# Gated expert rows added by scatter DMA straight into the output, tile by tile, in a two-stage FFN kernel

## The reference

```python
# stage A
h = gelu(x @ fc1_w.T + fc1_b)                      # 128 -> 512
y = concat([h @ fc2_w.T + fc2_b,                   # 96 shared outputs
            h @ experts_w[idx[seq]].T + experts_b[idx[seq]]])   # 32, one of 16 by sequence
# stage C
scores = y @ router_w.T                            # 8 experts
top_v, top_i = top_k(scores, 2);  w = softmax(top_v)
out = x + sum_e (gelu(y @ w1[e].T) @ w2[e].T) * w_e
```

## Time and profile before

| | us |
|---|---|
| median of 3 runs | 344.18 |
| lowest, highest | 340.74, 346.32 |
| span of the profiled execution | 320.1 |
| median minus span | 24.1 |
| POOL busy with the 64 scatters of stage A | 68.0 |
| POOL busy with the 80 scatters of stage C | 86.9 |

### The profile page before, as it was taken

One profiled execution on the slowest core, in us unless ns is written; L12 is line 12 of the kernel. 1 busy time (PEld: TensorE's weight loads), 2 busy tenths in 40 slices (PEclk: granted clock), 3 DMA queues, 4 the chain that ended last, 5 costly groups with the idle time before them and its releaser, 6 DMA issues.

```text
span 320.1 us, 5181 instructions
## 1 busy us (share of the span) xinstructions
PE 235.2 (73%) x1138; PEld 180.7 (56%) x1138; DVE 188.4 (59%) x471; ACT 178.5 (56%) x265; POOL 185.9 (58%) x203
## 2 busy tenths in 40 slices
PE   7974999979877326799999999798977979700000
PEld 2653776657655201578888888697856868600000
DVE  2568988578576470077776775465454665501880
ACT  4888577578461230296767666476555555401830
POOL 3009587777777774005776777565736656662660
PEclk9999799979979957699999999899999979955555
DMA  4395234329611153557775776847856664214981
GB/s 133 101 333 177 73 96 141 104 75 273 200 43 59 51 187 132 208 181 240 244 253 200 248 288 240 314 173 250 265 194 250 199 234 156 98 33 133 361 248 46
DMA packets 32611, 57.90 MB, mean 181 GB/s; under 512 B 5544, under 2 KB 15920, under 8 KB 32594
## 3 DMA queue, kind: packets, MB, share of 16 engines
q1 hardware_dynamic: 23778, 43.76, 39.1%
q0 software_dynamic: 4608, 8.54, 8.3%
q10 hardware_dynamic: 4208, 5.42, 6.0%
HBM read 20.56 MB, written 13.02 MB: 105 GB/s over the span
## 4 chain that ended last, share of the span: by engine, by line
PE 23%; issue 22%; POOL 22%; DMA 18%; DVE 5%; ACT 4%; SPq 3%; POOLq 1%; DVEq 0%; ACTq 0%
POOL slots L583 15%; PE hp L359 11%; DMA results<-rows,back_now 10%; PE dn L372 8%; POOL results L603 4%; DMA slots<-y_rows,slot 4%; PE dx L1069 2%; POOL ffn L624 2%; PE tr L1084 1%; DMA ffn<-results 1%; ACT hs L397 1%; ACT hid L387 1%; SPq L450 1%; DMA ffn_raw<-in_w2T 1%; DVE ffn L983 1%
## 5 line engine op out<-in xcount | busy, mean ns | idle before, releaser
L603 POOL DMA_INDIRECT results<-rows,back_now x80 | 86.9, 1086 | 49.6 <-POOL back_now L595 20.7
L583 POOL DMA_INDIRECT slots<-y_rows,slot x64 | 68.0, 1063 | 22.2 <-issue 20.1
L359 PE MATMUL hp<-xs,w 128*128 128x512 f32 (+1 forms) x288 | 66.7, 367 | 11.3 <-DVE xs L950 11.3
L406 DVE TENSOR_TENSOR hs<-hid,hs 128x1024 fp32r<-128x1024 f32 (+1 forms) x64 | 69.7, 1089 | 8.9 <-ACT hs L397 7.7
L387 ACT ACTIVATE hid<-hp 128x1024 f32<-128x1024 f32 (+1 forms) x48 | 42.4, 883 | 51.4 <-PE hp L359 45.5
L372 PE MATMUL dn<-hs,w 128*128 128x512 f32 (+1 forms) x288 | 67.6, 371 | 0.0
L359 PEld LDWEIGHTS hp<-xs,w 128*128 128x128 f32 x288 | 49.4, 192 | 22.4 <-issue 9.9
L397 ACT ACTIVATE hs<-hid 128x1024 fp32r<-128x1024 f32 (+1 forms) x64 | 60.9, 952 | 1.1
L372 PEld LDWEIGHTS dn<-hs,w 128*128 128x128 f32 x288 | 48.7, 194 | 7.5
L959 DVE COPY rows<-tr 128x512 f32<-128x512 f32 (+1 forms) x24 | 14.4, 602 | 34.2 <-POOLq L568 32.6
L359 PE MATMUL hp<-xs,fc 128*128 128x512 f32 x96 | 28.3, 436 | 0.0
(11 more groups left out here) (123 smaller groups left out, 246.6 us busy)
## 6 DMA issues: line engine op xcount, KB each, us to landing
w<-ffn SPq DMA_DIRECT2D x48, 512.0 KB, 3.7
ffn<-results SPq DMA_DIRECT2D x16, 256.0 KB, 5.5
picked<-slots ACTq DMA_DIRECT2D x14, 264.0 KB, 3.5
x_raw<-in_xT SPq DMA_DIRECT2D x8, 256.0 KB, 3.2
cexp_raw<-in_cexpT SPq DMA_DIRECT2D x32, 64.0 KB
out<-ffn SPq DMA_DIRECT2D x8, 256.0 KB, 3.9
results<-rows,back_now POOLq DMA_INDIRECT x80
picked<-slots ACTq DMA_DIRECT2D x8, 132.0 KB
```

The lines of the kernel that those rows point to most:

```text
L359: mm = pe.matmul(dst, weight[:, w, cols], xs[:, st.parity, v, 0:width], start=m == 0, stop=m == len(passes) - 1)
L406: dve.tensor_tensor(by_block(k, st, hs[:, st.parity, 1, g, :]), by_block(k, st, hid[:, g, :]), by_block(k, st, hs[:, st.parity, 0, g, :].b ...
L583: pool.indirect_dma_start(out=slots, out_offset=bass.IndirectOffsetOnAxis(ap=slot[:, u, n:n + 1], axis=0), in_=y_rows[:, u, k, r, :], in_o ...
L603: pool.indirect_dma_start(out=results, out_offset=bass.IndirectOffsetOnAxis(ap=back_now[:, u, r:r + 1], axis=0), in_=rows[:, u, r, :], in_ ...
```

## The change

The tensor results, the loads of it, the gating and the adding at the end go. out gets 512 spare rows (DUMP) behind the 4096 token rows; x is copied into out by a DMA after stage A's loads, and a zero tile into the spare rows. The gates are computed per chunk in stage A (ACT: tanh of half the gap; DVE: 0.5 - 0.5 tanh and its complement) and travel in the second extra column of each slot row; the row number is now the token's, the same for both choices, and padding rows name the spare rows. DVE multiplies each block by its gates on its way from PSUM. POOL's scatters add to the rows of out (compute_op=ALU.add). Since two tiles can hold the same token's two choices, all scatters of tile t-1 must have landed before the first of tile t: the wait moves from the middle of the tile to its start. The host cuts the spare rows off.

```diff
-NO_ROW = 1 << 24
+DUMP = RPT * P
+SUM_COLS = 2048
...
+    def whole(t):
+        return t[0:TOKENS, :].rearrange("(a b) d -> a (b d)", b=SUM_COLS // P)
...
             run_steps(sp, CHUNKS, step_a, ahead=2)
-            sp.wait_ge(s_pool_lo, POOL_EXP)
-            sp.dma_start(x_rows[:, :, :], x_all).then_inc(s_xrows, 16)
+            sp.dma_start(whole(out), x.rearrange("s (q b) d -> (s q) (b d)", b=SUM_COLS // P)).then_inc(s_sums, 16)
+            sp.wait_ge(s_zeros, 1)
+            sp.dma_start(out[TOKENS:TOKENS + DUMP, :].rearrange("(p r) d -> p (r d)", r=RPT), zeros[:, :])\
+              .then_inc(s_sums, 16)
...
             run_tiles(sp, step_c)
-            for u in range(2):
-                sp.wait_ge(s_zout[u], 16 * Step(TILES // 2 - 1, u).blocks_upto())
-            def load_z(g):
-                for k in range(TOPK):
-                    sp.dma_start(z_rows[:, g, k, :], result_groups[:, k, g, :])\
-                      .then_inc(s_z[g], 16)
-            for g in range(GROUPS):
-                load_z(g)
-            for g in range(GROUPS):
-                sp.wait_ge(s_fin, g + 1)
-                sp.dma_start(out_store[:, g * FIN_GROUP:(g + 1) * FIN_GROUP, :],
-                             z_rows[:, g, 0, :].rearrange("p (s d) -> p s d", d=P)).then_inc(s_out, 16)
...
+            pool.memset(zeros[:, :], 0.0).then_inc(s_zeros, 1)
...
-            pool.memset(filler[:, :, P:P + 1].bitcast(I32), NO_ROW).then_inc(s_filler, 1)
+            pool.iota(filler[:, :, P:P + 1].bitcast(I32), [[1, RPT], [0, 1]], base=TOKENS, channel_multiplier=RPT)\
+                .then_inc(s_filler, 1)
...
                 for r in range(st.blocks()):
-                    if r == st.blocks() // 2:
+                    if r == 0:
                         free_rows(st - 1, s_zout, (st - 1).blocks_upto(), s_zfree)
                         pool.sem_inc(s_go, 1)
                     pool.indirect_dma_start(
-                        out=results, out_offset=bass.IndirectOffsetOnAxis(ap=back_now[:, u, r:r + 1], axis=0),
-                        in_=rows[:, u, r, :], in_offset=None,
-                        bounds_check=TOPK * TOKENS - 1, oob_is_err=False).then_inc(s_zout[u], 16)
+                        out=out, out_offset=bass.IndirectOffsetOnAxis(ap=back_now[:, u, r:r + 1], axis=0),
+                        in_=rows[:, u, r, :], in_offset=None, compute_op=ALU.add).then_inc(s_zout[u], 16)
+            pool.wait_ge(s_sums, 16 * 2)
...
+                if (st - 2).within(CHUNKS):
+                    wait(act, s_gap, (st - 2).value + 1)
+                    act.activation(lean[:, :], gap[:, :], ACT.Tanh, scale=0.5).then_inc(s_lean, 1)
...
-            act.wait_ge(s_gap, 1)
-            act.activation(egap[:, :], gap[:, :], ACT.Exp).then_inc(s_exp, 1)
-            act.activation(warm[:, :], ones_f[:, 0:1], ACT.Gelu)
...
+                wait(dve, s_lean, st.value + 1)
+                for k in range(TOPK):
+                    dve.tensor_scalar(y_rows[:, st.parity, k, :, P + 1:P + 2].rearrange("p r w -> p (r w)"), lean[:, :],
+                                      k - 0.5, 0.5, ALU.mult, ALU.add)
                 dve.tensor_copy(slot[:, st.parity, :], slot_f[:, :]).then_inc(s_slot, 1)
...
-                    dve.tensor_copy(rows[:, done.parity, 0:blocks, :], tr[:, 0:blocks, :]).then_inc(C.rows, 1)
+                    for r in range(blocks):
+                        ins = dve.tensor_scalar(rows[:, done.parity, r, :], tr[:, r, :],
+                                                back[:, bass.ds(done.value, 1), r, 1:2].rearrange("p t w -> p (t w)").bitcast(F32),
+                                                None, ALU.mult)
+                    ins.then_inc(C.rows, 1)
...
-                    ins = dve.scalar_tensor_tensor(z0[:, r, :], z0[:, r, :], gate[:, 0, s:s + 1], x_rows[:, s, :],
-                                                   ALU.mult, ALU.add)
...
-    out = nc.dram_tensor("out", (SEQS, P, P), F32, kind="ExternalOutput").ap()
+    out = nc.dram_tensor("out", (TOKENS + DUMP, P), F32, kind="ExternalOutput").ap()
-    return r.results[0]["out"]
+    return r.results[0]["out"][0:TOKENS].reshape(SEQS, P, P)
```

More of the change, by code:

```diff
@@ L243, in build @@
         slot = sb("slot", [P, 2, RPT * TOPK], I32)
[L244 to L247, removed]
+        gap = sb("gap", [P, RPT])
+        lean = sb("lean", [P, RPT])
         count = sb("count", [P, EXP])
@@ L270, in build @@
         end_i = sb("end_i", [P, EXP], I32)
-        back = sb("back", [P, TILES, RPT], I32)
+        back = sb("back", [P, TILES, RPT, 2], I32)
         back_now = sb("back_now", [P, 2, RPT], I32)
@@ L312, in build @@
         s_zout = [sem(f"s_zout{n}") for n in range(2)]
[L313 to L316, removed]
+        s_zeros = sem("s_zeros")
         class Counts:
@@ L594, in send_back @@
                 blocks = st.blocks()
-                pool.tensor_copy(back_now[:, u, 0:blocks], back[:, bass.ds(t, 1), 0:blocks].rearrange("p t r -> p (t r)"))\
+                pool.tensor_copy(back_now[:, u, 0:blocks],
+                                 back[:, bass.ds(t, 1), 0:blocks, 0:1].rearrange("p t r w -> p (t r w)"))\
                     .then_inc(s_back, 1)
@@ L617, in _ @@
                 send_back(Step(i, 1))
[L620 to L627, removed]
+            for u in range(2):
+                pool.wait_ge(s_zout[u], 16 * Step(TILES // 2 - 1, u).blocks_upto())
         @block_ctx.scalar
@@ L680, in step_a @@
                         act_high(act, A, st, 0)
+                if (st - 2).within(CHUNKS):
+                    wait(act, s_gap, (st - 2).value + 1)
+                    act.activation(lean[:, :], gap[:, :], ACT.Tanh, scale=0.5).then_inc(s_lean, 1)
+                if st.within(CHUNKS):
                     if st.parity == 1:
@@ L731, in _ @@
             run_tiles(act, step_c)
[L734 to L745, removed]
         @block_ctx.vector
@@ L810, in choose @@
                 link_c(ins)
-                seqs = bass.ds(st.value * RPT, RPT)
-                dve.tensor_tensor(gap[:, seqs], top[:, :, 1], top[:, :, 0], ALU.subtract)
+                dve.tensor_tensor(gap[:, :], top[:, :, 1], top[:, :, 0], ALU.subtract).then_inc(s_gap, 1)
                 link_c(dve.tensor_tensor(
@@ L846, in step_a @@
                     wait(dve, s_yfree, done.value + 1)
-                    dve.tensor_copy(y_rows[:, done.parity, :, :, P:P + 1].bitcast(I32)
-                                    .rearrange("p k r w -> p (k r w)"),
-                                    result_row[:, bass.ds(done.value, 1), :, :].rearrange("p c k r -> p (c k r)"))
+                    for k in range(TOPK):
+                        dve.tensor_copy(y_rows[:, done.parity, k, :, P:P + 1].bitcast(I32).rearrange("p r w -> p (r w)"),
+                                        out_row[:, bass.ds(done.value, 1), :].rearrange("p c r -> p (c r)"))
                     dve.tensor_copy(y_rows[:, done.parity, 0, 0:RPT - 1, 0:P], three[:, :, 0:P])
@@ L935, in _ @@
             dve.tensor_scalar(owner_i[:, :], owner_f[:, :], float(EXP - 1), None, ALU.min).then_inc(s_where, 1)
[L938 to L941, removed]
             def split_picked(st):
@@ L947, in split_picked @@
                 width, blocks = C.width(st), st.blocks()
-                dve.tensor_copy(back[:, bass.ds(st.value, 1), 0:blocks].rearrange("p t r -> p (t r)"),
-                                picked[:, st.parity, 0:blocks, P:P + 1].bitcast(I32).rearrange("p r w -> p (r w)"))
+                dve.tensor_copy(back[:, bass.ds(st.value, 1), 0:blocks, :].rearrange("p t r w -> p (t r) w"),
+                                picked[:, st.parity, 0:blocks, P:P + 2].bitcast(I32))
                 dve.tensor_tensor(xs[:, st.parity, 1, 0:width], dx[:, 0:width],
```

32 lines of the change are left out of this document (6 added, 26 removed).

## The result

| | us |
|---|---|
| after: median of 4 runs (lowest, highest) | 392.37 (389.5, 396.91) |
| before, measured beside it: median of 4 runs | 342.46 (340.38, 346.32) |
| after : before | 1.1456, interval 1.1359 to 1.1553 |
| span of the profiled execution after, and its own time | 395.1, 396.91 |

Times are medians of all runs; a ratio compares the undisturbed runs alone, those within 1.5% of the fastest of their kernel.

A forecast was written before the change was run, and what follows sets the result against it. POOL bounds the router stage, PE the first expert tiles, then scatter landings. After: POOL's serial chain, 147.7 + 77.6 + 21.2 (23 handovers) + 3.5 + 24 L, span 343.6, +23.5 on 344.2 = 368 us; range 332 to 408.

The forecast's parts named there:

- L: Expert stage: time from a tile's last scatter's start until POOL sees it landed; 3.1 plain, 3.9 us adding, 24 times.
- the add's 0.8: Expert stage: the adding DMA's read of the old row lengthens each landing by 0.8 us.
- tail removed: End of kernel: loads of results, gating, adding and stores after the last scatter's landing go, 25.2 us.
- 56 steps inside tiles: POOL in the expert stage: scatter to next scatter within a tile, 1.386 us each, 77.6 us in all.
- Rival 4: POOL's scatters: issue of 0.97 us grows by half for all 80, +39 us, 407 us; chance 0.12.
- 1: Rival, expert stage: landings near the empty queue's value, L = 2.4, 332 us, faster; chance 0.13.
- 2: Rival, expert stage: empty-queue landing plus the added read, L = 2.8, 341 us, no difference; chance 0.12.
- 3: Rival, expert stage: loaded landing plus a whole trip of 1.1, L = 5.3, 401 us; chance 0.12.
- 5: Rival, ACT in the router stage: table loads around every tanh, two per chunk, +10 us, 378; chance 0.1.
- 6: Rival, PE in the expert stage: its clock falls when idle, 6.47 us per tile becoming 8.1 or 12.9; chance 0.03.
- The constant 24.1 us: Whole execution: 24.1 us lie around the profiled span of 320.1, making the three runs' median 344.18.
- The close: End of kernel: the program's close after the last landing, 3.5 us, stays.

The follow-up runs named there:

- b_wait0: The kernel before with only the wait for the previous tile's landings moved from mid-tile to ahead of its first scatter, plain scatters and old tail kept: 362.89 us.
- b_again: The kernel before, unchanged, profiled once more: 344.88 us, span 343.1.
- a_again: The kernel after, unchanged, run again on another chip: 368.64 us beside 322.44 for the kernel before, ratio 1.1432.
- a_plain: The kernel after with plain writes in place of the adding scatters, so the sum is left out: 347.01 us.
- a_plain_mid: The kernel after with plain scatters to distinct rows of a doubled out and the wait back in mid-tile, sum left out: 313.54 us, ratio 0.974.
- a_add_mid: The kernel after with adding scatters to distinct rows of a doubled out and the wait back in mid-tile, halves not summed: 339.02 us, ratio 1.0519.

## Why the prediction was right, and which terms were wrong

What was right is the mechanism: the tail goes, POOL's chain becomes serial, and the wait costs more than the tail gives. Split by the runs, with the prediction's own numbers in the middle column (the wait with L = 3.1, the add's 0.8 for each of 24 landings):

| part | predicted | measured | from |
|---|---|---|---|
| tail removed | -25.2 | -23.6 | 28.7 to 5.1 us |
| the wait at the tile's start, plain scatters | 173.2 - 144.1 = +29.1 | +25.3 | b_wait0 and b_again |
| the add, behind that wait | 24 x 0.8 = +19.2 | +46.8 | a_again 215.7 and a_plain 168.9 |
| stage A | +0.4 | not visible | a_again starts at 147.5, before at 147.3 |
| sum | +23.5 | +48.5 | measured as a whole: +49.9 and +46.2 |

With plain scatters the first two terms nearly cancel, as a_plain shows; nearly all of the loss is the add behind the wait, which the forecast put below the wait.

**The step that failed** is the term "56 steps inside tiles, each 1.086 us by the group's mean plus 0.30 = 1.386: 77.6 us". It took the adding scatter's issue to cost what the plain one's does. The step measures 1.92 us in the kernel after: from 172.33 to 386.66 are 214.3 us, 23 handovers of 4.65 take 107.0 of them, and 107.4 are left for 56 steps. That is 29.8 us more than forecast, and it is the whole gap of stage C (217.7 less the forecast 192.4 is 25.3; the handovers give 3.9 back and the last landing 0.6). With plain scatters the forecast of 1.386 holds: in a_plain the same count, 166.6 us less 23 handovers of 3.80, leaves 1.41. Rival 4 had named this, at 0.12: "POOL's issue is longer", with half of 0.97 more for all 80. The measured increase is 0.58, 60%. Its reason, two reads and a write for a row, was not tested. What the trace shows is one packet per row.

**L was right in size for the wrong reason.** Forecast from a scatter's start to its landing: 3.9. Measured: 3.3 for most, 3.7 as the mean that the handovers of 4.6 leave after 0.92. But the 0.8 put down to the add's read are 0.58 of issue and 0.3 of flight, and the 0.58 is paid in all 80 scatters and not in 24. The middle value for plain scatters, 3.1, stands against 2.9 in a_plain (3.80 less 0.92).

**The wait.** Right in place and nearly in size. The rows that the prediction named answer: 22 waits for landings (24 were forecast), 61.3 us in all, and handovers of 4.65 against about 4.8. Its cost also depends on the other part: 25.3 us with plain scatters, 215.7 - 179.8 = 35.9 with adding ones, since every longer issue then stands in the serial chain. In the same way the add costs 46.8 behind the early wait and 179.8 - 152.3 = 27.5 with the wait in mid-tile. Either change alone is less than half the sum.

**Rivals.** 1 and 2 (landings near the empty queue's) fell with the handovers: L is well over the break-even of 2.92, and in a_plain, where L is just under it, the time is indeed that of no difference (347.01 beside 341.11, within 2%). 3 (whole added trip, L = 5.3) fell as well. 5 fell with ACT's rows. 6: the granted clock went from 0.92 down to 0.78, but PE had room: the chain shown of a tile holds no piece of PE.

**Around the span.** The constant 24.1 us did not exist. It was stage A's stalls, absent in the one execution that was profiled. By luck they had nearly the same size in the runs of both kernels, so the sum was not hurt: stage C began 24.6 us later than forecast, and only 1.8 us lay around the span. **The close** of 3.5 us after the last landing measured 5.1. In the kernel before the last store had landed by 315.1, not at 316.6, and it was not the store that set the end but POOL's DRAIN. So the forecast of the tail, -25.2, had a wrong end; its miss of 1.6 is small because the DRAIN with adding scatters is shorter by 2.6.

**PE** fell to 71% of 200 to 260 and 60% of 260 to 320, as forecast ("near 60%"), then to 55%.

## What to carry to other kernels

Before an indirect DMA is made to add, price its issue: here it was 1.55 us instead of 0.97 for 128 rows of 512 bytes, paid on POOL for every one, while its flight grew by 0.3 only. Where accumulation also forces an order between tiles, the wait turns each issue into a part of the serial chain, so the two costs must be worked out together: the tail of 24 us was bought for 74. And a cheap share of such a tail may be had by scaling earlier and giving additions to the faster engine: 2.8% here, of which the traces explain about half.

## What was unexpected of the hardware

- The issue of an adding scatter costs POOL 60% more time (1.55 us against 0.97), and its rows go out as one packet each (13568 packets against 4608, at the same 9.58 MB).
- Tanh runs between Gelus with no table load, 0.20 us each.
- POOL's closing DRAIN takes 7.26 us after plain scatters (a_plain, a_plain_mid) and 4.64 after adding ones (after, a_again, a_add_mid). In the kernel before it ends 7.3 us after POOL's last addition, 4.8 us after the last store has landed, though the last scatter landed 28 us before. Why the two kinds differ stays open.
- In some executions the engines are held up in stage A for 1 to 10 us at a time, with nothing in the trace that ends it, in both kernels; stage C then starts 13 to 25 us later. In the piece of b_again from 52.35 to 60.13 PE and DVE do nothing and ACT 1.0 us of work, while POOL goes on.
